# Where GpSimd's row moves stand in two expert loops, and how long the memsets between them are

## The reference

```
gate_probs = softmax(x @ w_gate);  topk_vals, topk_idx = top_k(gate_probs, 2)
g, u = split(einsum('bsd,edh->ebsh', x, w_gate_up), 2)
expert_out = einsum('ebsf,efd->ebsd', silu(g) * u, w_down)
out = einsum('bse,ebsd->bsd', renormalised gates of the chosen two, expert_out)
```

## Time and profile before

| | us |
|---|---|
| median of 3 runs | 681.76 (680.92 to 682.18) |
| the profiled execution | 682.17, of which the span is 680.3 |
| PE busy | 576.5 (85% of the span) |
| DVE busy | 437.6 (64%) |
| ACT busy | 233.0 (34%) |
| POOL busy | 207.7 (31%) |

### The profile page before, as it was taken

How to read it: one execution, slowest core, us unless ns; L and a number is a source line. 1 busy time by engine, 2 the same in 40 slices (tenths; PEclk the granted TensorE clock), 3 DMA queues, 4 the chain that set the end, 5 groups by cost and what they waited for, 6 DMA issues and landing times.

```text
span 680.3 us, 12175 instructions
## 1 busy us (share of the span) xinstructions
PE 576.5 (85%) x3853; PEld 478.4 (70%) x3854; DVE 437.6 (64%) x1576; ACT 233.0 (34%) x515; POOL 207.7 (31%) x258
## 2 busy tenths in 40 slices
PE   5799817879997999999998679989996369999993
PEld 2477703769995568888987557746776159899993
DVE  8878883214365665566687686787778837555573
ACT  2355201235553423444433033325541013333331
POOL 6100057744557024920000000000000778733332
PEclk9899657979996999989989888989995579989997
DMA  9999922212254000000000350021000122211243
GB/s 220 184 185 248 267 75 63 67 52 72 71 151 141 0 2 1 1 1 1 1 0 1 119 129 1 1 82 44 1 1 0 52 59 62 62 47 47 56 123 112
DMA packets 61016, 47.67 MB, mean 70 GB/s; under 512 B 6266, under 2 KB 54819, under 8 KB 60806
## 3 DMA queue, kind: packets, MB, share of 16 engines
q1 hardware_dynamic: 56422, 37.68, 24.2%
q0 software_dynamic: 4544, 9.38, 4.1%
HBM read 27.53 MB, written 19.51 MB: 69 GB/s over the span
## 4 chain that ended last, share of the span: by engine, by line
PE 53%; issue 20%; SPq 12%; DVE 10%; another core or an unknown queue 2%; ACT 1%; DMA 1%; DVEq 0%; POOL 0%; POOLq 0%; ACTq 0%
PE bank L2186 16%; PE bank L2197 9%; PE bank L1826 7%; SPq L420 7%; PE bank L2008 5%; SPq L409 2%; SPq L414 2%; PE bank L1815 2%; PE bank L1816 2%; PE bank L1817 2%; PE bank L2174 2%; DVE X L1397 1%; DVE XW L991 1%; PE bank L1851 1%
## 5 line engine op out<-in xcount | busy, mean ns | idle before, releaser
L590 POOL DMA_INDIRECT xw<-XW,slot_i x64 | 62.4, 975 | 317.6 <-DVE slot_i L1149 296.7
L2186 PE MATMUL bank<-xT,wcur 128*128 128x128 f32 x936 | 124.5, 285 | 11.3 <-ACT xT L762 11.3
L2186 PEld LDWEIGHTS bank<-xT,wcur 128*128 128x128 f32 x936 | 117.3, 201 | 12.7 <-ACT xT L762 10.7
L606 POOL DMA_INDIRECT yt<-Y,dest_i x78 | 75.9, 973 | 90.0 <-ACT Y L775 44.6
L1257 DVE COPY wcur<-WA 128x512 f32 x78 | 37.8, 485 | 54.3 <-PE bank L2186 51.4
L1397 DVE SCALAR_TENSOR_TENSOR X<-bank,G,X 128x128 f32<-128x128 f32 x128 | 36.0, 344 | 47.4 <-PE bank L1826 38.7
L842 ACT ACTIVATE hT<-bank,b_cols 128x512 f32<-128x512 f32 x64 | 43.5, 687 | 65.7 <-PE bank L1817 65.2
L1826 PE MATMUL bank<-WC,hT 128*128 128x128 f32 x512 | 65.4, 283 | 0.0
L1826 PEld LDWEIGHTS bank<-WC,hT 128*128 128x128 f32 x512 | 62.6, 198 | 2.8 <-ACT hT L842 0.9
L1272 DVE TENSOR_TENSOR hT<-gb,bank 128x512 f32<-128x512 f32 x39 | 26.8, 688 | 44.5 <-ACT gb L767 38.6
L767 ACT ACTIVATE gb<-bank 128x512 f32<-128x512 f32 x39 | 23.3, 597 | 57.3 <-PE bank L2186 46.7
(11 more groups left out here) (390 smaller groups left out, 1142.4 us busy)
## 6 DMA issues: line engine op xcount, KB each, us to landing
xw<-pad_rows SPq DMA_DIRECT2D x34, 260.0 KB, 9.2
xrow<-xw SPq DMA_DIRECT2D x78, 65.0 KB
WA<-in_fc_dram SPq DMA_DIRECT2D x16, 256.0 KB, 6.5
YT<-yt SPq DMA_DIRECT2D x16, 256.0 KB, 2.9
WA<-in_pj_dram SPq DMA_DIRECT2D x8, 256.0 KB, 5.5
WB<-in_fc_dram SPq DMA_DIRECT2D x8, 256.0 KB, 4.6
WB<-in_pj_dram SPq DMA_DIRECT2D x8, 256.0 KB, 6.1
yt<-Y,dest_i POOLq DMA_INDIRECT x78
```

What stands on the lines that cost most here:

```text
L590: pool.indirect_dma_start(out=xw_dram, out_offset=bass.IndirectOffsetOnAxis(ap=slot_i[:, choice, tile:tile + 1], axis=0), in_=XW[:, tile, ...
L606: pool.indirect_dma_start(out=yt_dram, out_offset=bass.IndirectOffsetOnAxis(ap=dest_i[:, t:t + 1], axis=0), in_=Y[:, s, :], in_offset=None ...
L2186: ins = pe.matmul(dst, wcur[:, s4, at:at + P], xT[s4 % 2][:, :], start=True, stop=True)
```

## The change

`pause` becomes shorter (192 columns of 512, `PAUSE`), and it is the same in both layers. The eight moves of group 2 all stand ahead of the first put, each with a pause behind it. The first 24 puts (`PACED`) have a pause behind each, the other 15 none. Nothing else changes on POOL, and nothing on the other engines.

```diff
+PAUSE = 192
+PACED = 3 * YRING
...
-            def pause(layer, layers):
-
-                if layer in layers:
-                    link(pool.memset(M[:, 1, :], 0.0))
+            def pause():
+
+                link(pool.memset(M[:, 1, 0:PAUSE], 0.0))
...
                 for tile in range(GT, GT + GT // 2):
                     for choice in range(TOPK):
                         scatter(layer, 1, tile, choice)
-                        pause(layer, (0, 1))
+                        pause()
+                for tile in range(GT + GT // 2, TILES):
+                    for choice in range(TOPK):
+                        scatter(layer, 2, tile, choice)
+                        pause()
                 for t in range(SLOTS):
                     put(layer, t)
-                    if t < GT // 2:
-                        for choice in range(TOPK):
-                            pause(layer, (1,))
-                            scatter(layer, 2, GT + GT // 2 + t, choice)
-                        pause(layer, (1,))
+                    if t < PACED:
+                        pause()
```

## The result

The changed kernel is slower: 686.01 us median of 20 runs (683.59 to 688.73) against 681.65 us for the kernel before, measured beside it (20 runs, 674.5 to 686.54). The ratio is 1.008, with an interval of 1.006 to 1.010. The forecast was 668.3 us, faster.

A forecast was written before the change was run, and what follows sets the result against it. It took PE's chain as the bound, with two holes from POOL's dense indirect DMAs; 682.17 - 9.9 - 3.8 = 668.5 us, 668.1 against the median, so 668.3. Own range 666.5 to 671, 8 in 10 range 666.0 to 679.0.

The forecast's parts named there:

- What bounds the kernel: Both layers: PE's chain bounds, 1.89 and 2.79 us a slot, with holes where POOL's dense indirect DMAs hold up PE's semaphores.
- The distance of 1.50 us taken as harmless: POOL's paced indirect DMAs: 1.50 us apart, between harmful 1.26 and harmless 1.78, were taken to cost nothing.
- this stop counts, and not only the mean distance: POOL's pauses: waiting for its own memset brings POOL to a stop, which was chosen as what makes 1.50 us harmless.
- DVE's 4.02 us in layer 1: DVE's chain at 547.19, while POOL moves group 0 densely: 4.02 us late, cited as a sign that 1.26 is marginal.
- Nobody waits for either: no gain, no loss: POOL's groups 1 and 2: through 2.2 us sooner and landed at about 137 instead of 143, worth nothing.
- The old holes, 9.9 and 3.8 us: PE's chain at the dense DMA stretches: the holes go, gaining 9.9 us in layer 0 and 3.8 in layer 1.
- The first put: Layer 0: it starts at 135.1 and lands at 138.6, 3.2 us before ACT's copy of slot 8 needs the buffer.
- Rival 1: Both layers: part of the holes stays at 1.50 us, half the gain is lost, 675 us; chance 0.12.
- Rival 2: Layer 0: the first `setup1` on PE, not DMA density, makes the hole; 678 to 682 us, taken as 681; chance 0.07.
- Rival 3: Layer 0: 1.50 us is as bad as 1.26, 36 DMAs at 0.82 us cost 29.6; slower, 698 us; chance 0.11.
- Rival 4: Layer 1: DVE's copies at 1.27 instead of 0.42 us become the bound, costing 6 us, 674.5 us; chance 0.04.

The follow-up runs named there:

- the other occasion: The changed kernel run again, unaltered, beside the kernel before: 675.69 us against 681.01, ratio 0.9876.
- group 1 long: The changed kernel with 512 columns again in the eight pauses of group 1 only, in each layer: 667.46 us against 681.16, ratio 0.9789.

## Why the prediction was wrong

- *What bounds the kernel*: right as far as it went. On affected occasions dense indirect DMAs of POOL delay the semaphores; undoing and adding pauses moves the holes each time.
- *The distance of 1.50 us taken as harmless* is the step that failed, and with it the choice that "this stop counts, and not only the mean distance". The sum put the cost of this distance at nothing. It measured 10.5 and 10.0 us at the start of the two slot loops, against 9.1 and 5.0 gained, and on the other occasion 4.4 and 3.0 against 9.7 and 3.8. With a stop and 1.36 us the holes are there, and at 1.50 it depends on what came before and on the occasion. The prediction measured from a clean start: its dense stretch was the one from 126 us on. It didn't ask what group 0's 16 moves had left when group 1 began, though DVE's 4.02 us in layer 1 had the same mark. Nor was the start of the kernel before clean: its first copies came 5.1 us behind group 1's first move, 2 more than on a free occasion.
- *"Nobody waits for either: no gain, no loss"*, of group 1 being through 2.2 us sooner, failed in the same way. That nobody waits for the group's rows is true, but the 0.27 us taken from each of eight pauses had a use that no wait in the trace names. Given back, they bring the ratio to the kernel before from 1.008, or 0.988 on the other occasion, to 0.979.
- *The old holes, 9.9 and 3.8 us*: right as mechanism and nearly in size. The stretch from first to last copy lost 9.1 us in layer 0 and 5.0 in layer 1.
- *The first put*: forecast at 135.1, with 3.2 us to spare; it is at 135.69. It didn't bind, partly because slot 8 was late too. Where slot 0 was on time (group 1 long) layer 0 took 78.3 us from first to last copy against 74.2 on a free occasion, some 4 us which the forecast didn't have. They aren't the first put's: they come at slots 14 to 17, with late semaphores. So that kernel's 667.46 us, close to the forecast of 668.3, isn't the forecast's sum come true.
- *Rival 1*, part of the holes stays, has the price of the second occasion (675.69 against 675), and by luck: the old holes were wholly gone there, and new ones at the start of the slots took back 7.4 of the 13.5 us.
- *Rival 2*, `setup1`: refuted. In the kernel with group 1's long pause `setup1` stands where it did, and PE is busy 15.00 of 15 us.
- *Rival 3*, slower, had the right sign. Its price was per DMA, 0.82 us times 36, while most of the delay is paid once in each layer, at the start of the slots: 10.5 and 10.0 us. Nor is 1.50 as bad as a denser program: with 1.36 us everywhere the time is 697.20.
- *Rival 4*, DVE's copies: not seen. POOL has 80 short memsets instead of 28, and the mean of the copies of layer 0 and 1 is 462 ns, before 485, the longest 0.61 us, before 1.27. The rule that DVE and GpSimd share a port pair as an exclusive lock (the Trainium skill, SBUF — State Buffer, Who interferes with whom) didn't make the long copy the usual case:

```profile
L1260 DVE COPY wcur<-WA 128x512 f32 x78 | 36.0, 462 | 49.4 <-PE bank L2189 46.9
```

## What to carry to other kernels

A pause that seems to wait for nothing can be what lets a backlog go, so before shortening it ask what the work ahead of it has left, not only whether someone waits for the work behind it. When a resource that the trace doesn't show was harmful at one spacing and harmless at another, a spacing between them is to be tried at the busiest start, and its forecast should have both signs in it. Where one wait is late without a cause in the trace, look for a second engine with the same mark ("remote") and for the earliest place where it occurs: the cause lies there or ahead of it. And when a hole goes, look where the next dense stretch is, since with all pauses long it came back behind the last of them.

## What the runs showed of the hardware

- On affected occasions, while POOL issues indirect DMAs 1.26 or 1.36 us apart, semaphores between PE, ACT and DVE come up to 8.5 us late (in the kernel before slot 7's rows are turned at 131.71 and ACT copies them at 140.23). At 1.50 in the changed kernel, behind the dense group 0, ACT's copy starts 7.8 us behind PE's matmul of 0.5. At 1.78 or more, as long as it lasts, ACT's largest delay of this kind is the 2 us of the first copy. At 1.50 the backlog of group 0 stays, and after a good start layer 0 still loses 3 to 5 us. One stop of 3 us clears the start (first copy 3.5 us behind instead of 7.9). The backlog is a picture that fits the runs; no trace shows where the semaphores are held.
- DVE is hit as ACT is. In the changed kernel its first target rows wait 14.1 us in one piece for something that the trace doesn't see end, on free occasions 7.8 to 9.3:

```profile
DVE dest_i L1268 <- remote: 14.1, 1, 14.1
```

- It isn't there on every occasion. The same kernel before takes 681 us with it and 663 without. On seven of the eight free profiles the trace has a landing time for the puts (2.3 or 2.4 us, the median), on the eighth and on all affected ones it has none:

```profile
yt<-Y,dest_i POOLq DMA_INDIRECT x78, 2.3
```

```profile
yt<-Y,dest_i POOLq DMA_INDIRECT x78
```

What makes an occasion affected stays open.
